# The second feed-forward of a graph network kept on a row's own 64 columns, its pooling sums made inside the value products, and half of a dt matrix made by GpSimd

## The reference, cut to what matters

```
fx = (x @ W_fx.T + b_fx)...;  xm = (x @ W_x.T + b_x)...          # 8 heads of 64
sw = softmax((xm @ W_slice.T + b_slice) / temp)                  # node x slice, per head
snorm = sw.sum(2)
st = einsum('bhnc,bhng->bhgc', fx, sw) / (snorm + 1e-05)         # 64 tokens of 512 features
# the mixer, over the 64 tokens of one graph:
z, xBC, dt = split(st @ in_w.T)
dt = softplus(dt + dt_bias)                                      # 8 heads forward, 8 backward
x, B, C = silu(causal_conv(xBC))
h_t = h_{t-1} * exp(dt_t * -exp(A_log)) + dt_t * B_t * x_t;  y_t = C_t . h_t    # both directions
y = shift(y_fw) + shift(y_bw) + x * (x @ fcD_w.T + Dp)
yg = y * silu(z);  yg = yg * rsqrt(mean(yg^2) + 1e-5) * norm_w
ot = yg @ out_w.T
out = einsum('bhgc,bhng->bhnc', ot, sw) @ out_w.T + out_b
```

## Time and profile before

| what | value |
|---|---|
| runs | 3245.23, 3245.34, 3250.94 us |
| median | 3245.34 us |
| span of the profiled execution | 3243.7 us |
| busy share of the span | PE 80%, PEld 64%, DVE 70%, ACT 55%, POOL 27% |
| instructions | 68706 |

### The profile page before, as it was taken

One profiled execution on the slowest core, in us unless ns is written; L12 is line 12 of the kernel. 1 busy time (PEld: TensorE's weight loads), 2 busy tenths in 40 slices (PEclk: granted clock), 3 DMA queues, 4 the chain that ended last, 5 costly groups with the idle time before them and its releaser, 6 DMA issues. The chain is left out here.

```text
span 3243.7 us, 68706 instructions
## 1 busy us (share of the span) xinstructions
PE 2606.3 (80%) x19386; PEld 2087.8 (64%) x19386; DVE 2274.7 (70%) x6679; ACT 1783.4 (55%) x5130; POOL 867.6 (27%) x863
## 2 busy tenths in 40 slices
PE   5899996992776941789999999699996888759992
PEld 4577776992675941656776777566664555549992
DVE  6777774666685656667777777499997688835555
ACT  2344434663674532755565555377774777726664
POOL 0233334663343432300000000000001155534442
PEclk9899997996887975989999999799998999969996
DMA  5111112334321213200000000000001000012225
GB/s 200 46 59 59 59 34 76 84 84 127 125 77 48 66 59 118 82 1 1 0 0 0 0 0 1 22 21 21 24 19 67 5 28 28 29 42 65 63 62 175
DMA packets 142548, 168.55 MB, mean 52 GB/s; under 512 B 19920, under 2 KB 118224, under 8 KB 141776
## 3 DMA queue, kind: packets, MB, share of 16 engines
q1 hardware_dynamic: 116688, 118.67, 12.1%
q0 software_dynamic: 21504, 44.74, 4.0%
q10 hardware_dynamic: 4224, 3.59, 0.4%
HBM read 115.87 MB, written 51.05 MB: 51 GB/s over the span
## 5 line engine op out<-in xcount | busy, mean ns | idle before, releaser
L1198 POOL DMA_INDIRECT y_rows<-ffn_e_rows_out,ffn_e_scatter_at x352 | 339.7, 965 | 385.7 <-DVE ffn_e_rows_out L1226 218.4
L1340 PE MATMUL bank<-ffn_e_xT,ffn_e_mine 128*128 128x128 f32 x3360 | 439.6, 278 | 2.2 <-ACT ffn_e_xT L1272 1.4
L1340 PEld LDWEIGHTS bank<-ffn_e_xT,ffn_e_mine 128*128 128x128 f32 x3360 | 410.4, 195 | 3.4 <-ACT ffn_e_xT L1272 2.2
L722 POOL DMA_INDIRECT sorted_rows<-ffn_rows,ffn_slot x320 | 315.5, 986 | 278.8 <-issue 266.4
L1274 ACT ACTIVATE ffn_e_mine<-constants 128x512 f32 (+1 forms) x352 | 250.2, 712 | 114.6 <-issue 65.3
L1246 DVE TENSOR_TENSOR ffn_e_hid<-ffn_e_act,bank 128x256 f32<-128x256 f32 (+1 forms) x280 | 136.1, 486 | 225.0 <-ACT ffn_e_act L1300 199.8
L1350 PE MATMUL bank<-ffn_e_mine,ffn_e_hid 128*128 128x128 f32 x1968 | 278.0, 276 | 2.6 <-DVE ffn_e_hid L1250 2.4
L2566 ACT ACTIVATE gnn_prob<-bank,gnn_low 128x256 f32<-128x256 f32 x512 | 203.5, 501 | 107.1 <-DVE gnn_low L2480 107.1
L1350 PEld LDWEIGHTS bank<-ffn_e_mine,ffn_e_hid 128*128 128x128 f32 x1968 | 247.5, 192 | 5.3 <-DVE ffn_e_hid L1250 4.8
L1300 ACT ACTIVATE ffn_e_act<-bank 128x256 f32<-128x256 f32 (+1 forms) x280 | 120.9, 432 | 106.0 <-PE bank L1340 104.9
L2480 DVE TENSOR_REDUCE gnn_low<-bank 128x2 f32<-128x512 f32 x256 | 159.0, 684 | 24.1 <-PE bank L2665 21.3
(11 more groups left out here) (505 smaller groups left out, 6583.6 us busy)
## 6 DMA issues: line engine op xcount, KB each, us to landing
g_adj<-in_adjT SPq DMA_DIRECT2D x48, 512.0 KB, 4.0
ffn_e_rows_in<-sorted_rows SPq DMA_DIRECT2D x346, 66.0 KB
ffn_c_y<-y_rows SPq DMA_DIRECT2D x80, 256.0 KB, 3.2
g_adj_rows<-in_adj SPq DMA_DIRECT2D x16, 512.0 KB, 4.3
gnn_adj<-in_adjT SPq DMA_DIRECT2D x16, 512.0 KB, 4.0
constants<-in_ffn SPq DMA_DIRECT2D x1, 6281.0 KB, 22.2
y_rows<-ffn_e_rows_out,ffn_e_scatter_at POOLq DMA_INDIRECT x352, 2.2
constants<-in_ffn SPq DMA_DIRECT2D x1, 5204.0 KB, 15.4
```

Of the source, the lines that this page charges most:

```text
L722: eng.indirect_dma_start(c.sorted_rows, bass.IndirectOffsetOnAxis(r.slot[par][:, k, j:j + 1], 0), r.rows[par][:, j, :], None).then_inc(r.d ...
L1198: g.indirect_dma_start(c.y_rows, bass.IndirectOffsetOnAxis(scatter_at[par][:, k:k + 1], 0), rows_out[par][:, k, :], None).then_inc(scatter ...
L1340: ins = pe.matmul(chunk(part, ch), chunk(weights[:, i * HALF:(i + 1) * HALF], ch), x, start=True, stop=True)
```

## The change

Every token matrix keeps only a row's own 64 columns: rows 0 to 63 hold the first graph's columns and rows 64 to 127 the second's. The dt matrices, `dt_both`, `factor` and the decay become 128 x 8 x 64, the decay logarithms fit in one bank, and the C.B products and y become products of 64x64 blocks, each graph in its own part of the array. `own_masks` is the sum of the two halves of the masks, made once.

The value weights are laid out so that each 128-wide block has 64 columns of value weights and 64 columns of ones. One product over both graphs then gives numerators in one half of the partitions and denominators in the other; the products with a ones matrix go away. `pooled` now takes both graphs at once.

The forward half of the dt matrix moves from ScalarE to VectorE, the backward half from VectorE to GpSimd. The transposes of the softmax weights alternate between bank 0 and bank 7 (`SWT`), the last piece is split around the first half of y, and the second piece of the next turn's logits moves ahead of the z projection.

```diff
-                    g.wait_ge(norm_ps, t * 2 + 1)
+                    g.wait_ge(st_ps, now)
...
+                    g.wait_ge(dt_ready, t + 1)
+                    if not first:
+                        g.wait_ge(D_ps, now if first else counted(g, t))
+                    g.tensor_tensor(dt_run[:, 1], per_head(dt[:, HEADS2:], SL), own_masks[:, 1, None, :].broadcast_to([P, HEADS2, SL]),
+                                    ALU.mult).then_inc(dt_back_ready, 1)
                     g.wait_ge(xtok_ready, t + 1)
...
-                v.scalar_tensor_tensor(value_w[:], w["b_fx"], last_row, B[4][:], ALU.mult, ALU.add).then_inc(fused, 1)
+                for a in range(2):
+                    mine, bias = (ap.rearrange("p (k a s) -> p k a s", k=KC, a=2)[:, :, a, :] for ap in (B[4][:], w["b_fx"]))
+                    v.tensor_copy(value_w[:, a, :, (1 - a) * SL:(2 - a) * SL], ones[:, None, 0:SL].broadcast_to([P, KC, SL]))
+                    ins = v.scalar_tensor_tensor(value_w[:, a, :, a * SL:(a + 1) * SL], bias, last_row, mine, ALU.mult, ALU.add)
+                ins.then_inc(fused, 1)
+                v.tensor_tensor(own_masks[:], masks[:, :, 0:SL], masks[:, :, SL:], ALU.add)
...
+                def pooled(t):
+
+                    v.wait_ge(st_ps, t + 1)
+                    low_half, high_half = slice(0, SL), slice(SL, P)
+                    v.tensor_scalar(sn[low_half], B[5][high_half, :], 1e-5, None, ALU.add)
+                    then(v, v.tensor_scalar(sn[high_half], B[7][low_half, :], 1e-5, None, ALU.add), stn, 2 * t + 1)
+                    then(v, v.reciprocal(sn[:], sn[:]), stn, 2 * t + 2)
+                    tokens = stT[:].rearrange("p k g s -> p (k g s)")
+                    v.tensor_tensor(tokens[low_half], B[5][low_half, :], sn[low_half], ALU.mult)
+                    v.tensor_tensor(tokens[high_half], B[7][high_half, :], sn[high_half], ALU.mult).then_inc(stT_ready, 1)
...
-                    a.wait_ge(dt_ready, t + 1)
-                    for hd in range(HEADS2):
-                        ins = a.activation(dt_run[0][:, hd, :], masks[:, 0, :], ACT.Copy, scale=dt[:, hd:hd + 1])
-                    ins.then_inc(dt_fwd_ready, 1)
...
+                    a.wait_ge(D_ps, t + 1)
+                    for hd in range(HEADS2):
+                        one = B[6][:, hd * SL:(hd + 1) * SL]
+                        ins = a.activation(one, one, ACT.Exp, scale=neg_a[:, hd:hd + 1])
+                    ins.then_inc(D_exp, 1)
...
+                def pool_values(t):
+
+                    pe.wait_ge(ph_ready, t * 2 + 2)
+                    wait_past(pe, swT_ready, t * TT)
+                    for a in range(2):
+                        for j in range(KC):
+                            cols = slice((2 * j + a) * SL, (2 * j + a + 1) * SL)
+                            ins = mm(B[5 + 2 * a][:, j * P:(j + 1) * P], value_w[:, a, j, :], pooled_h[:, :, cols], start=True, stop=True)
                     ins.then_inc(st_ps, 1)
...
+                    def product_y(g):
+                        rows_ = slice(g * SL, (g + 1) * SL)
+                        for hd in range(HEADS2):
+                            cols = slice(hd * HD2, (hd + 1) * HD2)
+                            ins = mm(B[5][rows_, cols], decay[rows_, hd, :], xtok[rows_, cols], start=True, stop=True)
+                        return ins
+                    wait_past(pe, swT_ready, t * TT + 2)
+                    swT_part(par, 3, (0, 1))
+                    product_y(0)
+                    swT_part(par, 3, (2, 3)).then_inc(swT_ps, 1)
+                    product_y(1).then_inc(y_ps, 1)
```

More of the change, by code:

```diff
@@ L1899, in phase_ffn2 @@
             "dtr", "u", "m", "e", "e2", "r", "s", "s2", "poly", "dt"))
-        gm, g_both = sb("gm", [P, 2, P]), sb("g_both", [P, P])
+        own_masks, gm, g_both = sb("own_masks", [P, 2, SL]), sb("gm", [P, 2, SL]), sb("g_both", [P, SL])
         xtok = sb("xtok", [P, IN2])
-        dt_run = [sb(f"dt_run{i}", [P, HEADS2, P]) for i in range(2)]
-        dt_both, factor = sb("dt_both", [P, HEADS2, P]), sb("factor", [P, HEADS2, P])
-        decay = [c.spare["ffn2"][:, q * 4 * P:(q + 1) * 4 * P].rearrange("p (h t) -> p h t", h=4) for q in range(2)]
+        dt_run = sb("dt_run", [P, 2, HEADS2, SL])
+        dt_both, factor, decay = (sb(n, [P, HEADS2, SL]) for n in ("dt_both", "factor", "decay"))
         g8, term, yg, yn = sb("g8", [P, HEADS2]), sb("term", [P, IN2]), sb("yg", [P, IN2]), sb("yn", [P, IN2])
@@ L2097, in turn @@
                     v.wait_ge(dt_both_ready, t + 1)
-                    v.tensor_tensor(factor[:], dt_both[:], g_both[:, None, :].broadcast_to([P, HEADS2, P]), ALU.mult).then_inc(factor_ready, 1)
+                    v.tensor_tensor(factor[:], dt_both[:], g_both[:, None, :].broadcast_to([P, HEADS2, SL]), ALU.mult).then_inc(factor_ready, 1)
                     if more:
@@ L2101, in turn @@
                     v.wait_ge(factor_ready, t + 1)
[L2102 to L2105, removed]
+                    v.wait_ge(D_exp, t + 1)
+                    v.tensor_tensor(decay[:], heads(B[6][:]), factor[:], ALU.mult).then_inc(decay_ready, 1)
                     if not first:
@@ L2240, in lg_piece, with swT_part @@
                     mm(LG[k % 2][:], hT[:, k * P:(k + 1) * P], logit_w[:], start=True, stop=True).then_inc(lg_ps, 1)
+                def swT_part(par, k, chunks):
+                    for j in chunks:
+                        ins = pe.transpose(SWT[k % 2][:, j * P:(j + 1) * P], sw[par][:, k, j * P:(j + 1) * P], c.ident[:])
+                    return ins
                 def swT_piece(t, par, k, pm_turns=None):
@@ L2246, in swT_piece @@
                         wait_past(pe, pm_ready, 2 * t)
-                    wait_past(pe, swT_ready, t * TT + k)
-                    for j in range(KC):
-                        ins = pe.transpose(B[0][:, j * P:(j + 1) * P], sw[par][:, k, j * P:(j + 1) * P], c.ident[:])
-                    ins.then_inc(swT_ps, 1)
+                    if k == 1:
+                        pe.wait_ge(stT_ready, t + 1)
+                    wait_past(pe, swT_ready, t * TT + k - 1)
+                    swT_part(par, k, range(KC)).then_inc(swT_ps, 1)
                 def tail_y(t):
@@ L2366, in turn @@
                     pe.wait_ge(sz_ready, t + 1)
+                    for k in range(KC):
+                        mm(B[4][:, 2 * P:2 * P + HEADS2], xT[:, k, :], fcd[:, k, :], start=(k == 0), stop=(k == KC - 1))
                     for d in range(2):
[L2368 to L2370 removed]
+                        for g in range(2):
+                            ins = mm(B[4][g * SL:(g + 1) * SL, d * SL:(d + 1) * SL], Bt[:, g * SL:(g + 1) * SL],
+                                     Cpad[:, 2 * d + g * SL:2 * d + (g + 1) * SL], start=True, stop=True)
                     ins.then_inc(G_ps, 1)
@@ L2374, in turn @@
                     pe.wait_ge(dt_back_ready, t + 1)
-                    for half in range(2):
-                        for d in range(2):
-                            ins = mm(B[6 + half][:], masks[:, 1 - d, :], dt_run[d][:, half * 4:half * 4 + 4, :].rearrange("p a n -> p (a n)"),
-                                     start=(d == 0), stop=(d == 1))
-                        ins.then_inc(D_ps, 1)
+                    for d in range(2):
+                        ins = mm(B[6][:], masks[:, 1 - d, :], dt_run[:, d].rearrange("p h n -> p (h n)"), start=(d == 0), stop=(d == 1))
+                    ins.then_inc(D_ps, 1)
                     swT_piece(t, par, 2)
```

68 lines of the change are left out of this document (16 added, 52 removed).

## The result

| | before | after |
|---|---|---|
| median of the runs, measured together, us | 3245.75 | 3294.87 |
| span of the profiled execution, us | 3243.7 | 3293.2 |
| phase ffn2 in it, us | 706.2 | 755.0 |

The ratio is 1.0149, with an interval from 1.0135 to 1.0164: the changed kernel is 49 us slower. The forecast was 3247, with a range up to 3264. All but 0.7 us of the 49.5 in the span lies in the one phase that the change touches.

A forecast was written before the change was run, and what follows sets the result against it. TensorE's queue sets the turn before; afterwards the loop through VectorE and ScalarE does. Stretches sum to -0.09 a turn, -1.4 in 16; setup +1.3 gives median 3245.2, one more clock fall +1.75 gives 3247 us, range 3232 to 3264.

The forecast's parts named there:

- The sum of the work: Second feed-forward turn: five stretches of the loop added up, -0.09 us a turn, -1.4 in 16 turns.
- GpSimd's block: xT to fourth exponential: GpSimd's backward dt half blocks VectorE's Bt, charged 0.78 us (bounds 0 and 1.04).
- The rival without a block: GpSimd does not block VectorE: second stretch 1.94, turn -0.78, with setup and one fall 3236 us; 24%.
- the second stretch: xT to the fourth softmax exponential: 3.42 us before, 2.60 expected, a gain of 0.82.
- Narrow passes: 64x64 products of y and G on TensorE: 0.056 us a pass, 0.90 for each half of y.
- the fourth stretch: y to the end of yg: 3.51 us before, 4.13 expected, a loss of 0.62.
- The fifth stretch: yg to the next first minimum: 12.63 us before, 12.46 expected, a gain of 0.17.
- The first stretch: First minimum to xT: 16.49 us, same instructions, expected unchanged.
- near 4.6 us: TensorE's saving of 41 us a turn: ones-matrix pooling sums, half the decay logarithm passes and the 1.18 transpose wait go.
- The prediction's own sign of being wrong: Wrong if Bt stays at 0.28, y takes over 3 us, or most turns have mean clock 0.96 or less.
- I take one more fall than before, +1.75: TensorE's granted clock: sparser stretches around y, xT and G bring one more fall to 1.2 GHz, +1.75 us in all.
- The clock falls in most turns: Rival: ten falls of TensorE's clock instead of three, 7 x 1.75 = 12.3 us, giving 3258; 28%.

The follow-up runs named there:

- e4: The changed kernel with the backward half of the dt matrix made by VectorE instead of GpSimd; 3291.90 us.
- e1: The changed kernel with unread products in all four TensorE waits: ahead of xT, Cpad, the decay matrix and the gated output; 3250.99 us.
- e2: The changed kernel with unread products in the first three TensorE waits alone, ahead of xT, Cpad and the decay matrix; 3268.90 us.
- e3: The changed kernel with six unread products in the last TensorE wait alone, between y and the pooling; 3275.64 us.
- e9: The changed kernel reordered, both dt halves on VectorE, plus six unread products between y and the pooling; 3213.30 us.
- e5: The kernel before with the new pooling alone (pooling sums inside the value products, one reciprocal of 512 columns); 3260.47 us.

## Why the prediction was wrong, step by step

**The sum of the work held, to 0.33 us a turn.** Against the turn at full clock (boundaries as in the prediction; a stretch that ends at y ends here at the transposes put ahead of it):

| stretch | expected, us | measured, us |
|---|---|---|
| first minimum to xT | 16.49 | 1603.11 - 1586.88 = 16.23 |
| xT to the fourth exponential | 2.60 | 1605.77 - 1603.11 = 2.66 |
| fourth exponential to y | 5.48 | 1611.20 - 1605.77 = 5.43 |
| y to the end of yg | 4.13 | 1615.58 - 1611.20 = 4.38 |
| yg to the next first minimum | 12.46 | 1628.37 - 1615.58 = 12.79 |
| turn | 41.16 | 41.49 |

- GpSimd's block: Bt was expected at 1.06 us (0.28 + 0.78), and took 1.13 (it was 0.28 in the kernel before). The rival without a block is out. What it gave for the second stretch, 1.94, is right for a kernel without GpSimd's step: in e4 the stretch is 1.93.
- Narrow passes: within y they start 0.058 us apart (0.056 expected), and each change of division cost 0.09, as taken from the earlier trace rows. From a half's first pass to the next instruction it is 1.07 (1611.54 to 1612.61), where 0.99 was expected. Of the 0.25 of the fourth stretch the two halves make about 0.15, and the two pairs of transposes, slower than expected, 0.08.
- Decay exponentials 1.72 (1.75 expected), reciprocal 3.35 (3.4). The fifth stretch is 0.33 longer; 0.2 of it is VectorE's pooling, 6.2 instead of 6.0, since its halves of 64x512 do not overlap.
- The first stretch was expected unchanged and is 0.26 shorter, mostly since the two instructions behind VectorE's softmax divisions start 0.11 earlier each; why is open. It makes up for part of what the fourth and fifth lose, and that was not foreseen.
- The "near 4.6 us" that TensorE is spared adds up to 4.8 from its own terms (1.72 + 1.93 + 1.18); the time does not go by it.
- The waits of TensorE came where they were expected: stT 1.00, xT 0.84, Cpad 0.69, the decay matrix 1.33, and 1.56 behind y. The prediction's own sign of being wrong, most turns at a mean clock of 0.96 or less, came true.

**The step that failed is the last term, "I take one more fall than before, +1.75".** The prediction had both thin stretches in hand ("a second sparse one around xT and G") and still priced one fall more in 16 turns. By the rows the 14 turns lost 617.9 - 14 x 41.50 = 36.9 us to the clock, against 582.6 - 14 x 41.25 = 5.1 before: 31.8 of the 35.3 us by which they grew; the work's 0.25 a turn is the other 3.5. That the clock is the cause, and that the thinned stretches bring it down, is shown by e1, e2, e3 and e9: the falls go where the waits are filled. The remaining 13.5 us of the phase lie in its setup and first turn (80.5 to 88.6 us, clock 0.83 to 0.75) and its tail (43.1 to 48.5, 0.92 to 0.83), which no experiment took apart; the prediction had 1.3 us there, for the setup.

**The rival was right in kind and short in size.** "The clock falls in most turns" had 28% and gave 3258. It counted ten falls at one place for 1.75 each. There were two places in a turn, 1.09 and 1.70 us, both hit in nine of the 14 turns and one of them in three more. What would have led there: the old turn stood at the edge, with falls in three turns, one of them in the earlier trace rows, and the change makes that stretch thinner and adds another. At such an edge a step that thins every turn alike should have been priced in every turn as the far case: by the prediction's own price, two places in 16 turns less the three falls of before are 29 x 1.75 = 51 us, and the range should have reached that far up. (That the measured loss is 49 is in part luck: the first place costs 1.09 and not 1.75.) The profile of before couldn't tell that it would come to that, but it could tell that the price per fall was known and the number was not.

**The gain that the change might have brought** (less work on all three engines) went into waits: TensorE was busy 38.5 us of a turn at full clock before and 36.1 after. The turn didn't follow, since it was set by the loop; and the waits, with the thin work between them, took the clock away. The Trainium skill (TensorE: Matmul & The Clock Gate, A second HAM failure mode: psum-queue depth-cycling) describes a kernel whose frequent short idle gaps between groups of products make the clock go up and down; this trace agrees, with no wait longer than 1.56 us in a turn that loses 2.8.

What stays open: which property of a stretch decides. TensorE's busy time doesn't sort them: 2.71 of 3.40 us stood ahead of a fall (1689.80) and 2.08 of 3.41 ahead of none (1607.85). Whether the narrow passes count for less than wide ones was not settled either; e5 shows that falls come without them, e1 and e9 that with full waits they hardly come in spite of them (in two of 14 turns, and in none).

## What to carry to other kernels

Taking work off TensorE where another engine's loop sets the pace turns it into waits, and short waits of about a microsecond can cost more than the change spares: here the dense products behind them ran at 1.2 GHz. If a profile of before shows even a few falls in otherwise equal turns, price a thinning change with a fall at every thin stretch of every turn. What helped here was to put real work into the waits first, by order (3237.95 us), and unread products into what was left (3213.30).

## What was not expected of the hardware

- TensorE's clock fell in 13 of 14 turns although the longest wait in a turn was 1.56 us; 16 unread products a turn took the kernel from 49 us above the kernel before to 7.
- The fall hits the work behind the thin stretch, not the stretch itself: the eight pooling passes took 5.37 us instead of 3.67, while y just ahead of them kept its 1.14 a half.
- GpSimd's 128x512 product took 1.42 us beside VectorE, and a VectorE instruction of 0.28 us beside it took 1.13.
